# First aggregation: the sum of a block's counts stands two blocks ahead in VectorE's order; high parts of the first layer's main weights are made on ScalarE

## The reference

```
xn = _layernorm(x)
x = x + _L0_gnn_ref(xn, edge_index, L0_gnn_W, L0_gnn_b) + _L0_mix_ref(xn[None], ...)[0]
x = x + _L0_ffn_ref(_layernorm(x)[None], ...)[0]
# _L0_gnn_ref: self edges are added to (row, col)
h = jnp.einsum('nd,od->no', x, W) + b
deg_inv_sqrt = deg ** (-0.5)
msg = (deg_inv_sqrt[row] * deg_inv_sqrt[col])[:, None] * h[col]
out = jax.ops.segment_sum(msg, row, num_segments=num_nodes)
# _L0_mix_ref, 16 heads of 64: relu instead of softmax
q, k, v = jnp.split(x @ W_qkv, 3, axis=-1)
out = jnp.einsum('bhij,bhjd->bhid', jax.nn.relu(dots), v)
normed = (out - mu) / jnp.sqrt(var + EPS) * gamma + beta
return normed @ W_out + b_out
```

## Time and profile before

| what | value |
|---|---|
| median of three runs | 2449.43 us |
| profiled execution | 2450.88 us, span 2448.8 us |
| PE busy | 2183.0 us, 89% |
| POOL busy | 1237.5 us, 51% |
| DVE, ACT busy | 1277.2 us, 677.0 us |
| granted PE clock, mean | 0.944 |

### The profile page before, as it was taken

One profiled execution on the slowest core, in us unless ns is written; L12 is line 12 of the kernel. 1 busy time (PEld: TensorE's weight loads), 2 busy tenths in 40 slices (PEclk: granted clock), 3 DMA queues, 4 the chain that ended last, 5 costly groups with the idle time before them and its releaser, 6 DMA issues.

```text
span 2448.8 us, 41495 instructions
## 1 busy us (share of the span) xinstructions
PE 2183.0 (89%) x16776; PEld 1484.3 (61%) x16776; DVE 1277.2 (52%) x2114; ACT 677.0 (28%) x996; POOL 1237.5 (51%) x833
## 2 busy tenths in 40 slices
PE   6999989999949799896779998998999999995998
PEld 5565464555447666663334556774877877884765
DVE  5754525535848599884333372243645544265332
ACT  4144414434612222231003141220211212042332
POOL 6788888888876411103441277203425332731554
PEclk8999999999979899998889999998999999996999
DMA  3211232223353300013000011220100100347886
GB/s 127 87 19 37 70 87 56 74 56 94 111 142 117 102 18 18 18 64 130 18 18 1 26 35 44 62 79 26 53 27 26 51 17 27 108 167 259 154 152 112
DMA packets 91851, 176.88 MB, mean 72 GB/s; under 512 B 20921, under 2 KB 60992, under 8 KB 85286
## 3 DMA queue, kind: packets, MB, share of 16 engines
q1 hardware_dynamic: 74838, 145.63, 18.0%
q0 software_dynamic: 16848, 28.91, 7.1%
HBM read 120.83 MB, written 53.50 MB: 71 GB/s over the span
## 4 chain that ended last, share of the span: by engine, by line
PE 52%; POOL 28%; DVE 8%; issue 7%; DMA 3%; ACT 1%; DVEq 0%; SPq 0%; POOLq 0%; ACTq 0%
PE ps L477 12%; PE ps L479 12%; PE ps L480 12%; POOL edges_sorted L1433 8%; POOL WR L1376 3%; POOL WR L1423 3%; POOL WR L1419 3%; POOL WR L1372 3%; POOL WR L1422 3%; POOL WR L1369 3%; PE ps L849 3%; PE pt L849 2%; DVE SR L1704 2%; DVE SR L1816 1%; PE ps L1094 1%
## 5 line engine op out<-in xcount | busy, mean ns | idle before, releaser
L477 PE MATMUL ps<-WR,RB 128*128 128x256 f16 (+2 forms) x2120 | 600.9, 283 | 29.7 <-DVE SR L1704 22.8
L479 PE MATMUL ps<-WR,RB 128*128 128x256 f16 (+2 forms) x2120 | 600.2, 283 | 0.0
L480 PE MATMUL ps<-WR,RB 128*128 128x256 f16 (+2 forms) x2120 | 599.6, 283 | 0.0
L1369 POOL TENSOR_TENSOR WR<-WR,units 128x2048 f32<-128x2048 f32 (+2 forms) x36 | 147.9, 4108 | 475.9 <-PE ps L477 452.0
L477 PE MATMUL ps<-RB,WR 128*128 128x512 f16 (+1 forms) x720 | 247.7, 344 | 24.8 <-POOL WR L1376 9.9
L477 PEld LDWEIGHTS ps<-WR,RB 128*128 128x128 f16 x2120 | 209.4, 99 | 76.2 <-issue 16.5
L479 PE MATMUL ps<-RB,WR 128*128 128x512 f16 (+1 forms) x720 | 247.7, 344 | 0.0
L480 PE MATMUL ps<-RB,WR 128*128 128x512 f16 (+1 forms) x720 | 247.6, 344 | 0.0
L480 PEld LDWEIGHTS ps<-WR,RB 128*128 128x128 f16 x2120 | 209.3, 99 | 43.3 <-issue 1.7
L479 PEld LDWEIGHTS ps<-WR,RB 128*128 128x128 f16 x2120 | 209.6, 99 | 41.2 <-issue 1.3
L1433 POOL DMA_INDIRECT edges_sorted<-SR x160 | 189.0, 1181 | 55.7 <-issue 55.7
(11 more groups left out here) (339 smaller groups left out, 4225.1 us busy)
## 6 DMA issues: line engine op xcount, KB each, us to landing
WR<-in_w_moe SPq DMA_DIRECT2D x64, 256.0 KB, 3.4
moe_split<-WR SPq DMA_DIRECT2D x128, 128.0 KB, 1.8
RB<-moe_split SPq DMA_DIRECT2D x8, 2048.0 KB, 13.4
WR<-in_w_mix SPq DMA_DIRECT2D x12, 1024.0 KB
WR<-in_w_mix SPq DMA_DIRECT2D x8, 1536.0 KB
RB<-in_x SPq DMA_DIRECT2D x18, 512.0 KB, 6.1
WR<-in_w_out SPq DMA_DIRECT2D x8, 1024.0 KB
counts<-RB SPq DMA_DIRECT2D x1, 6400.0 KB, 16.5
```

Of the source, the lines that this page charges most:

```text
L477: m = nc.tensor.matmul(o, ah, bh, start=(k == 0), stop=False)
L479: nc.tensor.matmul(o, ah, bl, start=False, stop=False)
L480: m = nc.tensor.matmul(o, al, bh, start=False, stop=(k == n - 1))
L1369: ch.link(g.tensor_tensor(w, w, units[:, 2:3].to_broadcast([128, width]), ALU.mult))
```

## The change

In slots 2 to 12 ACT now makes the high part from the unscaled weights (its own factor 256), and then scales the weights in place for POOL, which is left with the low part. ACT does both behind tile 1 of the slot before (`weights_high`), and waits there for the load. In the aggregation the sum L1854 becomes `both(i)`, apart from `make(i)`: two sums stand ahead of the first `make`, and `both(i + 2)` stands right behind `make(i + 1)`. The pieces' counts after the slots become 5, 7, 9, 7, 10, 14 and 12.

```diff
+        def weights_high(act, n):
+            act.wait_ge(slot_begun, n)
+            act.wait_ge(w_loaded, 16 * n + 16)
+            w = wst[:, 0:2048]
+            nc.scalar.activation(wh[n % 2][:, 0:2048], w, ACT.Copy, scale=WS).then_inc(w_high, 1)
+            act.wait_ge(w_high, 2 * n - 3)
+            nc.scalar.activation(w, w, ACT.Copy, scale=WS).then_inc(w_high, 1)
...
             for i in range(NT):
                 v0_act_one(act, d, T, i)
+                if i == 1:
+                    weights_high(act, 3 * d + 1)
...
+                    if t == 1:
+                        weights_high(act, 3 * (p // 2) + 2 + p % 2)
...
-        PIECE_END = {0: 0, 1: 5, 2: 11, 3: 19, 4: 24, 5: 32, 6: 46, 7: PIECES}
+        PIECE_END = {0: 0, 1: 5, 2: 12, 3: 21, 4: 28, 5: 38, 6: 52, 7: PIECES}
...
             split(1, 1, 2048)
+            def low_part(n):
+                pool.wait_ge(w_high, 2 * n - 2)
+                split_low(n % 2, 2048)
             for n in range(2, 12):
-                split(n, n % 2, 2048)
+                low_part(n)
...
-            split(12, 0, 2048)
+            low_part(12)
...
+            def both(i):
+                dve.wait_ge(turn_done, r0 + 2 * i - 2)
+                v.tensor_tensor(z[i % 2], Bc[:, 2 * i], Bc[:, 2 * i + 1], ALU.add).then_inc(z_ready, 1)
+
             def make(i):
-                s = i % 2
-                dve.wait_ge(turn_done, r0 + 2 * i - 2)
-                v.tensor_tensor(z[s], Bc[:, 2 * i], Bc[:, 2 * i + 1], ALU.add).then_inc(z_ready, 1)
                 dve.wait_ge(turn_done, r0 + 2 * i + 1)
...
+            both(0)
+            both(1)
             make(0)
             for i in range(NT - 2):
                 make(i + 1)
+                both(i + 2)
                 put(i, 0)
                 put(i, 1)
                 stat1(i)
```

More of the change, by code:

```diff
@@ L298, in build_program @@
         w_split = sem("w_split")
+        w_high = sem("w_high")
         slot_begun = sem("slot_begun")
```

## The result

The changed kernel takes 2361.51 us (median of 3 runs, 2359.07 to 2362.39) where the kernel before takes 2449.43: a ratio of 0.964, 95% interval 0.962 to 0.966, so 88 us less. The prediction was 2365.4, with a range of 2351 to 2388.

A forecast was written before the change was run, and what follows sets the result against it. PE, busy 89% of the span, was taken as the bound, so its idle time counts. Terms 12.2 + 24 + 47.8 + 0 = 84.0 us off 2450.88 gave 2366.9, with the median 1.45 lower: 2365.4, range 2351 to 2388.

The forecast's parts named there:

- Slots, 12.2: Attention, heads of slots 7 and 10: POOL's low parts come in time, saving 10.55 and 1.66 us, together 12.2.
- The margin at slot 10: Attention: slot 10's low part ends near 489.8, PE is through slot 9 at 494.8, so 5 us early.
- ScalarE, nothing: Attention: 22 new ScalarE operations of 1.90 us, 42 us more of ACT, cost PE nothing.
- Early stretch, 0 between 8 and -4: Slots 1 and 2: PE's 5.0 us wait on DVE may shrink or grow; 8 gained to 4 lost, taken as 0.
- the rival with more gain: Slot 1's scan freed of POOL gains 8 us and lnO keeps 27.8: 96 us off, 2354 us; chance 0.13.
- lnO, 24: Start of lnO: the stall for the bias goes, first sum 27.8 us earlier, of which 24 stay (21 to 27.8).
- Aggregation, 47.8: Aggregation: PE's waits for the sum go, rounds fall from 20.34 to 14.35 us; 47.8 us off.
- a sign of being wrong: Aggregation, profile after: PE waiting for POOL's low part of a block would mean one large term falls.
- Behind it, 0: Stretch behind the aggregation, to the kernel's end: 0 us predicted.
- no other wait took the sum's place: Aggregation rival: POOL's split makes the low part late, a round takes 17 us, costing 19: 2384 us; chance 0.10.
- the bias and slot 10 were in time: Rival: norm's chain or bias later, lnO gives 10, late slot 10 takes 6: 2385 us; chance 0.12.
- no load held ScalarE: Attention rival: ACT waits for late loads behind slots 6, 9 or 11; all three make 2492 us; slower, chance 0.03.

The follow-up runs named there:

- agg_alone: The kernel before with only the aggregation's new order of the sum, two blocks ahead: 2396.97 us, ratio 0.978.
- bias_early: The kernel before with only the DMA of the bias issued earlier, beside gamma and beta, ahead of the last eight pieces: 2449.55 us, ratio 0.999.
- act_doubled: The changed kernel with ScalarE making the high part of slots 2 to 4 three times instead of once: 2358.03 us, one run.
- pieces_later: The changed kernel with the first five pieces moved from behind slot 2's low part to behind slots 3 and 4: 2352.69 us, one run.
- evac_interleaved: The changed kernel with DVE's wide operations on the edges' positions put between the evacuations of slot 2's tiles: 2375.97 us, ratio 0.967.
- weights_alone: The kernel before with only the weights' half (ScalarE's high parts and scaling, new table of pieces), old order of the sum: 2414.50 us, ratio 0.985.
- after_again: The changed kernel itself run once more as a control, nothing edited: 2362.07 us, ratio 0.962.
- old_table: The changed kernel with the old shares of the pieces, 18 instead of 12 behind slot 12's low part: 2364.11 us, ratio 0.964.
- sum_behind_puts: The changed kernel with both(i + 2) moved behind both puts, ahead of the statistics: 2410.44 us, ratio 0.982.
- both_edits: The changed kernel with slot 16's split moved behind lnO's last block and DVE's wide operations between slot 2's evacuations: 2344.14 us, ratio 0.955.

## Why the prediction was right

- *Slots, 12.2:* exact, 10.55 and 1.66, and in part by luck. Forecast and shift are read against the same one trace of before; agg_alone and bias_early have the same slots, and there slot 4's low part is late too, by 1.5 and 2.0 us, so that against them the slots give 15 us. The margin at slot 10 was mis-sized: 0.7 us instead of 5, because seven of the ten pieces wait 0.25 to 2.5 us for their loads and the ten take some 4.3 us each, not 3.84.
- *ScalarE, nothing:* shown by the constant shift through the slots and by act_doubled; the 1.90 us was measured.
- *Early stretch, 0 between 8 and -4:* -0.7, right on the number and not on the mechanism. The scan did get free of POOL (6.83 us instead of 10.10), as the rival with more gain had it, but that bought nothing: DVE's next chain waits for tiles that PE and ScalarE deliver at the same time in both kernels (it starts at 89.8 before and 89.9 after). And what the earlier pieces meet is not the wide operations, which take 7.7 us instead of 8.5, but the small ones ahead of them: the first wide one starts at 95.3 instead of 92.5. pieces_later and evac_interleaved show that the 8 us at the upper bound were there to be had, but not from this change.
- *lnO, 24:* 24.3 at the load of slot 14, by the steps foreseen (bias no longer last, norm's chain next, POOL's split on the small operations); the first sum ends 27.9 us earlier, where 27.8 were worked out. The stretch behind it gives 1.8 back, so that 22.5 reach the aggregation; that loss is not a fixed one, since by the same instructions weights_alone brings 22.9 there and after_again 26.4. bias_early shows that the stall belonged to POOL's queue; old_table that it was the lost work, not the new shares, that freed it, and that the pieces have some 9 us in hand before the bias is late (13.1 us later, they make it 3.9 late).
- *Aggregation, 47.8:* 51.6, the mis-sized term. All PE's waits for the sum went; at the first gather 3.3 us of waiting stayed under other names, as "the beginning doesn't move" had it. One of them is a wait for POOL's low part, which the prediction had named as a sign of being wrong; it was there before, with the sum's, and no later block has one. A round is 14.04, not 14.35: the transposes take 1.09 from start to start, where I took 1.30 from a round whose clock was already falling (1.50 us in all), and handing over costs nothing. And a round of before is 20.48 on the mean of seven, where I had taken five. That is 7 x 0.44 = 3.1 of the 3.8; the rest is at the last block, 2.5 instead of 2.0. The nearest low part is 3.0 us early, POOL's at 1199.15, wanted behind the turn of 1203.68, and what I had feared is in the trace, harmless: DVE's diagonal beside POOL's split.

```profile
1193.67 4.02 DVE L1721 SCALAR_TENSOR_TENSOR SR<-ident,deg,SR 128x128 f32<-128x128 f32 x1
...
1203.88 0.75 DVE L1721 SCALAR_TENSOR_TENSOR RB<-ps,deg,RB 128x512 f32<-128x512 f32 x1 [4.12 <-PE ps L481]
```

- *Behind it, 0:* 2.9 more, two drops of the clock that didn't come. They come in all four kernels whose aggregation still has waits (before, bias_early, weights_alone, sum_behind_puts: 1134.5 to 1134.7 us from the aggregation's end to the kernel's) and stay away in eight of the ten whose aggregation has none (1131.4 to 1131.8), so they hang on the aggregation's half; but in agg_alone and act_doubled the clock falls at other waits and it is 1135.3 and 1135.5. What decides it, no run shows.

The misses are +3.8, +2.9, -1.5 and -0.7, and sum to the 4.5 us between 84.0 and 88.5. Two traces of the same kernel (the changed one and after_again) differ by 0.5 us at slot 3 and by 3.9 more through lnO and the counting, so the -1.5 and the -0.7 can be chance. None of the rivals came: no other wait took the sum's place, the bias and slot 10 were in time (slot 10 by 0.7 us), and no load held ScalarE.

## What to carry to other kernels

An operation that depends on old data but stands in an engine's order behind a wait on new data is late by that wait; moved ahead of the wait it was free here at both places tried (between the puts is as good as ahead of both), and a round's price is then read from the pitch of its instructions. Where an engine idles for a DMA, look what else would have held it at that moment: here issuing the DMA earlier was worth 2.5 us at most, and taking the work off POOL's queue 24. And where the page's totals hide it, ask which engine's wide operations run beside which: of the two improvements that together beat both kernels one moves POOL's work out of a chain, and one lets DVE serve PE between wide operations.

## What the runs showed of the hardware

- A wait of PE of one length, 2.24 us, behind the same work, drops the clock in three rounds of eight (granted clock 0.91 over the round instead of 1.00), and each drop costs 1.66 us more; behind the waits of 3.82 to 4.96 us of before every round has some, 1.9 to 2.8 us. So the low clock behind a wait is not a fixed part of its price.
- DVE's operations in SBUF stretch beside POOL's: a scan of 125x3200 takes 10.10 us beside POOL's wide operation and 6.83 without, some of 125x20 take 0.87 to 1.03 beside pieces and 0.18 without, and one of 128x128 takes 4.02 us instead of 0.35. The scan ends 6.7 us, its own time, behind POOL's operation; the small ones end within 0.2 us behind the POOL operation beside them, whatever their own size. So a small one can take eleven times its own time (4.02 against 0.35), where the wide one takes half as much again.
- Stalls of 0.3 to 1.8 us of ScalarE, DVE and PE "for issue" in the attention, 21 to 28 us in all, came in all four kernels run on one chip and in none of the kept traces from the others (but for two of 0.3 us of DVE in both_edits); their cause is open.
